# Cross attention and a routed feed-forward block: the attention loop's order of scores, maxima and projections

## The reference

```python
x = x + xattn(layernorm(x), ctx, ctx, mask, w_q, w_k, w_v, w_o)
x = x + ffn(layernorm(x), ...)          # causal attention, router, 2 of 8 experts

def xattn(q, k, v, mask, w_q, w_k, w_v, w_o):
    query, key_, value = (split_heads(t @ w.T) for t, w in ((q, w_q), (k, w_k), (v, w_v)))
    query, key_ = _rope(query), _rope(key_)
    scores = einsum('bhqd,bhkd->bhqk', query, key_) / sqrt(DK)
    scores = where(mask[:, None, None, :] == 0, -10000.0, scores)
    x = einsum('bhqk,bhkd->bhqd', softmax(scores), value)
    return merge_heads(x) @ w_o.T
```

## Time and profile before

| what | value |
| --- | --- |
| median of 3 runs | 823.15 us (822.39 to 824.36) |
| span of the profiled execution, first to last instruction | 808.3 us |
| around the span, against that median | 14.9 us |
| mean granted TensorE clock over the span | 0.940 |
| TensorE busy, of the span | 706.0 us, 87% |
| VectorE busy | 557.3 us, 69% |
| ScalarE busy | 485.6 us, 60% |
| GpSimd busy | 355.8 us, 44% |
| first score of g0 | 86.6 us from the span's start |
| start of the last score of g127 | 522.8 us |
| granted clock 0.5 inside the loop | 90.5 to 107.6, 216.8 to 220.2 and 411.3 to 418.2 us |

### The profile page before, as it was taken

How to read it: one execution, slowest core, us unless ns; L and a number is a source line. 1 busy time by engine, 2 the same in 40 slices (tenths; PEclk the granted TensorE clock), 3 DMA queues, 4 the chain that set the end, 5 groups by cost and what they waited for, 6 DMA issues and landing times. The chain is left out here.

```text
span 808.3 us, 13262 instructions
## 1 busy us (share of the span) xinstructions
PE 706.0 (87%) x4318; PEld 425.8 (53%) x4318; DVE 557.3 (69%) x924; ACT 485.6 (60%) x940; POOL 355.8 (44%) x262
## 2 busy tenths in 40 slices
PE   3246899999899999899999899888978889999996
PEld 2242434443344443435334333276767778999986
DVE  5949777778777778778878884248996515555553
ACT  2010556777576778567766678856655136676673
POOL 4964605358006277005749991000035723544444
PEclk9775689999999999999989999999998799999999
DMA  9676264868655666114777872039925646633321
GB/s 258 213 224 165 84 240 124 229 155 271 206 158 173 176 187 239 58 45 119 224 260 262 276 273 79 1 93 358 344 53 135 256 108 141 120 35 40 33 32 20
DMA packets 59718, 130.71 MB, mean 162 GB/s; under 512 B 8869, under 2 KB 26309, under 8 KB 58197
## 3 DMA queue, kind: packets, MB, share of 16 engines
q1 hardware_dynamic: 33364, 72.86, 27.6%
q0 software_dynamic: 16848, 35.95, 17.6%
q10 hardware_dynamic: 9440, 21.06, 9.0%
HBM read 80.80 MB, written 69.39 MB: 186 GB/s over the span
## 5 line engine op out<-in xcount | busy, mean ns | idle before, releaser
L757 DVE TENSOR_REDUCE mx<-wide 128x2 f32<-128x1024 f32 x256 | 305.6, 1223 | 89.0 <-PE wide L928 88.4
L616 ACT ACTIVATE probs<-narrow 128x512 f32<-128x512 f32 x488 | 267.3, 601 | 94.4 <-PE narrow L966 92.6
L966 PE MATMUL narrow<-qst,kst 51*128 51x512 f32 x488 | 182.9, 464 | 4.2 <-ACT probs L616 3.5
L928 PE MATMUL wide<-kst,qst 49*128 49x512 f32 x512 | 159.7, 476 | 21.4 <-DVE mx L757 9.4
L966 PEld LDWEIGHTS narrow<-qst,kst 51*128 51x128 f32 x488 | 78.9, 190 | 147.3 <-ACT probs L616 94.7
L981 PE MATMUL values<-probs,vaug 128*17 128x512 f32 x1024 | 139.2, 616 | 1.4 <-ACT probs L616 0.8
L1735 POOL DMA_INDIRECT out<-res,token x39 | 61.2, 1569 | 91.7 <-DMA out<-res,token 60.2
L928 PEld LDWEIGHTS wide<-kst,qst 49*128 49x128 f32 x512 | 68.6, 198 | 43.7 <-DVE mx L757 28.0
L462 POOL TENSOR_TENSOR turn_b<-turn_a,tab 128x1024 f32<-128x1024 f32 x10 | 24.2, 2420 | 115.3 <-ACT turn_a L610 114.8
L1267 POOL DMA_DIRECT2D out<-xt x4 | 5.5, 1376 | 108.1 <-DVE xt L1462 108.1
L1760 ACT ACTIVATE h_hi<-narrow 128x512 fp32r<-128x512 f32 x39 | 23.3, 598 | 42.2 <-PE narrow L1840 42.2
(11 more groups left out here) (281 smaller groups left out, 1310.4 us busy)
## 6 DMA issues: line engine op xcount, KB each, us to landing
list_rows<-in_w ACTq DMA_DIRECT2D x56, 342.0 KB, 5.5
kst<-k_pieces SPq DMA_DIRECT2D x14, 784.0 KB
k_pieces<-turn_a SPq DMA_DIRECT2D x16, 512.0 KB, 5.2
w_hi<-w_hi SPq DMA_DIRECT2D x16, 512.0 KB, 11.0
w_lo<-w_lo SPq DMA_DIRECT2D x16, 512.0 KB, 11.8
turn_a<-in_w POOLq DMA_DIRECT2D x11, 512.0 KB, 5.7
w_hi<-turn_b POOLq DMA_DIRECT2D x11, 512.0 KB, 3.0
w_lo<-turn_a POOLq DMA_DIRECT2D x11, 512.0 KB, 4.6
```

The source lines that it names most:

```text
L616: nc.scalar.activation(probs[:, n % NP, :], score_bank(n), ACT.Exp, scale=DK ** -0.5).then_inc(exp_done, 1)
L757: last = nc.vector.tensor_reduce(mx[quad % 2][:, qt, :, hp, kh], slot[:, :, :], axis=AX.X, op=ALU.max)
L928: last = nc.tensor.matmul(slot[:, i, :], qst[u % 3][r:r + R_MAX, h, P * qt:P * qt + P], kst[u % 3][r:r + R_MAX, h, 512 * kh:512 * kh + 512 ...
L966: nc.tensor.matmul(score_bank(n), kst[u % 3][r:r + R_ALL, h, P * kt:P * kt + P], qst[u % 3][r:r + R_ALL, h, :], start=True, stop=True).the ...
```

## The change

The order inside a group becomes s0, maximum, s1, weigh of g-1, s2, maximum, s3, then all other jobs; every group up to g116 has two maxima (g0 three, g117 none), and the last maxima of a quad end 3 groups before it for all quads. The estimated costs and `place` are gone. q, k, v and oP inside the loop come in halves of 256 columns, one to a group. xn, and the pieces of the turned attention, get buffers of their own (`xn`, `aT_hi`, `aT_lo`); the mask's two small tiles move into `attn` to make room. The unused `begin` and `finish` are taken out. In SP's queue the store of the turned queries goes ahead of the second max rows, and the loads of queries and keys ahead of the third.

```diff
-def lead(quad):
-    return 3 + 0.25 * max(quad - 5, 0)
-GROUP_COST = 2.3
-JOB_COST = {"q": 1.4, "k": 1.4, "v": 1.4, "oP": 1.4, "xT": 1.0, "oT": 1.0, "out": 0.5}
 AHEAD = 4
+LEAD = 3
...
-    for t in range(1, B):
-        g = 32 * (t - 1)
-        timed += [(g + 5.8, ("xn", t)), (g + 7, ("xT", t)), (g + 8.5, ("q", t, 0)), (g + 10, ("q", t, 1)), (g + 10, ("rope", t, 2))]
-        timed += [(g + x, ("v", t, n // 2, n % 2)) for n, x in enumerate((11.5, 13.5, 15, 16.5))]
-    for t in range(2, B):
-        g = 32 * (t - 2)
-        timed += [(g + 14.5, ("c", t, 0)), (g + 17.5, ("c", t, 1))]
-        timed += [(g + x, ("k", t, n // 2, n % 2)) for n, x in enumerate((18.5, 21, 23.5, 26))] + [(g + 21, ("rope", t, 0)), (g + 26, ("rope", t, 1))]
+    for b in range(B):
+        g, t = 32 * b, b + 1
+        if t < B:
+            timed += [(g, ("xn", t)), (g + 0.5, ("xT", t))]
+            timed += [(g + x, ("q", t, n // 2, n % 2)) for n, x in enumerate((3, 4, 6, 7))] + [(g + 7.5, ("rope", t, 2))]
+            timed += [(g + 13.2 + n, ("v", t, n // 4, n // 2 % 2, n % 2)) for n in range(8)]
+        if t + 1 < B:
+            timed += [(g + 16.5, ("c", t + 1, 0)), (g + 20.5, ("c", t + 1, 1))]
+            timed += [(g + 21.2 + n, ("k", t + 1, n // 4, n // 2 % 2, n % 2)) for n in range(8)] + [(g + 24.5, ("rope", t + 1, 0)), (g + 28.5, ("rope", t + 1, 1))]
+        if b > 0:
+            timed += [(g + 2.2, ("oT", b - 1))] + [(g + x, ("oP", b - 1, n // 2, n % 2)) for n, x in enumerate((8, 10, 11, 12))]
...
-    for b in range(B - 1):
-        g = 32 * b + 32
-        timed += [(g + 2.2, ("oT", b)), (g + 3.5, ("oP", b, 0)), (g + 5.5, ("oP", b, 1))]
...
-        first, last = when(max(8 * (quad - 1) - lead(quad - 1), 0)), when(8 * quad - lead(quad))
+        first, last = max(8 * (quad - 1) - LEAD, 0), 8 * quad - LEAD
...
-        timed += [(place(first + (last - first) * n / (len(todo) - 1)), j) for n, j in enumerate(todo[:-1])] + [(place(last) + 0.6, todo[-1])]
+        timed += [(first + (last - first) * n / (len(todo) - 2), j) for n, j in enumerate(todo[:-2])] + [(last - 0.01, todo[-2]), (last + 0.1, todo[-1])]
...
+        steps = [("score", 4 * g)] + [("job", j) for j in tops[:1]] + [("score", 4 * g + 1)] + [("weigh", g - 1)] * (g > 0)
+        steps += [("score", 4 * g + 2)] + [("job", j) for j in tops[1:2]] + [("score", 4 * g + 3)]
+        return steps + [("job", j) for j in tops[2:] + rest]
...
-    attn = sb("attn", [P, QT, D])
-    xn = attn
-    aT_hi, aT_lo = xT_hi, xT_lo
+    attn, xn = sb("attn", [P, QT, D]), sb("xn", [P, QT, D])
+    aT_hi = sb("aT_hi", [P, KC, SQ], F32R)
+    aT_lo = sb("aT_lo", [P, KC, SQ], F32R)
+    mask_i, mask_s = attn[0:B * KT, 0, 0:P].bitcast(I32), attn[0:B * KT, 1, 0:P]
...
             if t < B:
                 load_keys(2 * t)
+                store_turned(t, 2)
             load_max_rows(4 * b + 2)
             if t < B:
-                store_turned(t, 2)
+                load_queries(2 * t)
             if t + 1 < B:
                 load_context(t + 1, 1)
             if t < B:
-                load_queries(2 * t)
-            load_max_rows(4 * b + 3)
-            if t < B:
                 load_queries(2 * t + 1)
                 load_keys(2 * t + 1)
+            load_max_rows(4 * b + 3)
...
+                cols = columns(j[3:])
+                return product(slot[:, cols], weight("q", slice(P * j[2], P * j[2] + P)), transposed("xT", cols))
```

More of the change, by code:

```diff
@@ L33, with final @@
 HALF = 64
-def lead(quad):
-    return 3 + 0.25 * max(quad - 5, 0)
-GROUP_COST = 2.3
-JOB_COST = {"q": 1.4, "k": 1.4, "v": 1.4, "oP": 1.4, "xT": 1.0, "oT": 1.0, "out": 0.5}
 AHEAD = 4
+LEAD = 3
+def final(order, *begin):
+    return next(j for j in reversed(order) if j[:len(begin)] == begin)
 def attention_order():
@@ L67, in attention_order @@
     for quad in range(QUADS - 1):
-        timed.append((8 * quad + 9.3, ("out", quad)))
+        timed.append((8 * quad + 9.1, ("out", quad)))
     timed += [(GROUPS - 12.8, ("oT0", B - 1)), (GROUPS - 9.5, ("oP0", B - 1))]
-    for b in range(B - 1):
-        g = 32 * b + 32
-        timed += [(g + 2.2, ("oT", b)), (g + 3.5, ("oP", b, 0)), (g + 5.5, ("oP", b, 1))]
-    lengths = [GROUP_COST + sum(JOB_COST.get(j[0], 0) for t, j in timed if int(t) == g) for g in range(GROUPS)]
-    begins = [sum(lengths[:g]) for g in range(GROUPS + 1)]
@@ L108, in attention_order @@
     after += [("root0", 0), ("again0", 0), ("root0", 1), ("rates0", 0)]
-    order = before + [j for now in steps for what, j in now if what in ("job", "finish")] + after
+    order = before + [j for now in steps for what, j in now if what == "job"] + after
     index = {j: n for n, j in enumerate(order)}
@@ L112, in attention_order @@
     for b in range(1, B):
-        assert index[("xT", b)] < index[("out", 4 * (b - 1))]
-        assert b < 2 or index[("oT", b - 2)] < index[("xn", b)] and index[("oP", b - 2, 1)] < index[("xT", b)]
-        assert index[("q", b, 1)] < index.get(("oT", b - 1), len(order))
-        assert all(index[("v", b - 1, g, 1)] < index[("c", b, g)] for g in range(2))
+        assert index[("xT", b - 1)] < index[("xn", b)] and index[final(order, "q", b - 1)] < index[("xT", b)]
+        assert all(index[final(order, "v", b - 1, g)] < index[("c", b, g)] for g in range(2))
+        assert b < 2 or index[final(order, "oP", b - 2)] < index.get(("oT", b - 1), index.get(("oT0", b - 1)))
     return order, index, before, steps, after
@@ L230, in cross_attention @@
     for now in group_steps:
-        ring += [("score", j) if what == "score" else j for what, j in now if what == "score" or what in ("begin", "job") and in_ring(j)]
+        ring += [("score", j) if what == "score" else j for what, j in now if what == "score" or what == "job" and in_ring(j)]
     ring_no = {j: n for n, j in enumerate(ring)}
@@ L602, in job @@
                     act.wait_ge(pv_done, 32 * (b - 1))
[L603 to L604 removed]
+                kts = range(4 * g + 2 * n, 4 * g + 2 * n + 2)[slice(j[4], j[4] + 1) if j[4:] else slice(0, 2)]
+                dst, src = vaug[b % 2][:, kts.start:kts.stop, :, 0:DK], slot[:, columns(j[4:])].rearrange("p (k h d) -> p k h d", k=len(kts), h=H)
             else:
@@ L647, in _ @@
                     exponential_of_pair(g)
-                elif what in ("job", "finish"):
+                elif what == "job":
                     job(j)
@@ L821, in _, with product @@
         pe.wait_ge(ident_in, 16)
-        def product(out, left, right, part=None):
+        def product(out, left, right):
             passes = [(a, c, k) for a, c in ((0, 0), (0, 1), (1, 0)) for k in range(KC)]
             for n, (a, c, k) in enumerate(passes):
-                if part is None or n // KC in part:
-                    last = nc.tensor.matmul(out, left(a, k), right(c, k), start=n == 0, stop=n == len(passes) - 1)
+                last = nc.tensor.matmul(out, left(a, k), right(c, k), start=n == 0, stop=n == len(passes) - 1)
             return last
```

117 lines of the change are left out of this document (43 added, 74 removed).

## The result

The changed kernel is slower: 835.62 us median of 4 runs (830.53 to 838.24) against 822.77 (821.71 to 824.36), a ratio of 1.0169 with a 95% interval of 1.0129 to 1.0208. The forecast was 818.3, its range ended at 832.

The account below looks back on a forecast made before the run. Plain groups were taken as bound by a ring of weigh, scores and exponentials between TensorE and ScalarE, projection groups by TensorE. The parts summed to -4.8 us on the 823.15 us median, giving 818.3, range 804 to 832.

Parts of the forecast that it names:

- Part 4: xn and xT one behind the other at three places: two groups take 9.6 us instead of 5.3, in all +4.4.
- Part 8: Max rows queued behind stores of turned keys: late by 2.5 us at g32 and 1.2 at g64, +2.7.
- Part 9: TensorE's clock in the loop: three short low spells at xT, +1.5 us, between 0 and +13.6.
- what would show it: Signs to check in the new trace; a low clock in over 25 us of the loop would disprove the clock term.
- Rival (c): TensorE's stands of 2.5 us at xT bring low-clock spells of 17 us: 830.4 us, chance 0.12.
- Part 1: New order in a group: plain groups 2.65 instead of 2.59 us, +7.0; a slot saved at low clock, -1.7.
- Part 2: q, k, v projections in halves: 52 times 0.57 us instead of 26 times 1.32, -4.7; such a group takes 3.22.
- Part 3: Output's projection at batch ends: transposes 1.75 us, four quarters 1.05 each; three times -2.05, so -6.1.
- Part 5: Groups with out: 14 cost 15.5 us before; after, nine alone cost 1.05 each, five with a half 0.65: -2.8.
- Part 7: The loop's tail: last maxima come two groups later, so two more groups aren't paired, +0.9 us.
- Part 6: Maxima spread evenly over groups: less TensorE waiting for reductions, -6.0 us, between 0 and 12 taken back.
- 14.9 us around the span: Difference between before's 823.15 us median and its 808.3 us profiled span, taken as lying around the span and staying.

Follow-up runs that it names:

- xn_rows: Changed kernel with xn moved to where GpSimd is idle and each fourth quad's max row put ahead of the query and key loads: 804.90 us, 0.9811 of before.
- no_cast: xn_rows with the 16 small casts of the negated maxima computed as a second reduction: 802.43 us, 0.9739 of before.
- rows_first: Changed kernel with each batch's fourth-quad max row put back ahead of the loads of queries and keys: 826.37 us, 1.0068 of before.
- old_weave: xn_rows with each group's steps in the order of the kernel before: 843.97 us, 1.0260 of before.
- before_again: The kernel before, unedited, run again for a second profile: 820.25 us, ratio 1.0017 to before.
- xn_two_ahead: xn_rows with xn of batches 2 and 3 two groups ahead of their transposes, inside GpSimd's rotations again: 812.82 us, 1.0039 of before.

## Why the prediction was wrong

By its own parts:

- **Part 4, xn and xT, failed, and decided the sign.** The step was "the four normalisations take 1.37", a duration from a place where GpSimd was idle, carried to a place where it isn't. The two groups were to take 9.6 us; they took 17.5, 14.1 and 16.4, 19.2 us more in all three places together, part of it at the lower clock. Without the stand (xn_rows) they take 8.3, 7.6 and 8.0. The Trainium skill ("SBUF — State Buffer", Who interferes with whom) has the rule that would have told it: VectorE and GpSimd share one pair of SBUF ports as an exclusive lock for a whole instruction, and on VectorE's side copies, casts and tensor_scalar between SBUF tiles can take it, as does anything with two SBUF inputs against a GpSimd instruction that reads, while tensor_reduce never does. The traces agree in all four. Beside GpSimd tensor_scalar took up to 2.50 us instead of 0.40, the cast up to 2.14 instead of 0.18, the subtraction of two SBUF tiles up to 1.88 in no_cast instead of 0.18, and the reductions 0.19 and 1.21 to 1.23, as they do alone. Rows of the kernel before, the cast at 1.78 above, would have told it too.
- **Part 8, late rows, was mis-sized and in the wrong place.** I put 2.5 us at g32 and 1.2 at g64, for stores of turned keys; from these terms, less the 0.64 of before, the term is 3.1 and not the 2.7 written. The wait at g32 was 1.2 and there was none at g64. All such waits are 8.2 us: 5.9 of it at g24 (3.4), g56 (1.1) and g88 (1.4), the fourth quads of their batches, whose rows I had moved behind the loads without a price, and 1.2 at g104, whose cause is open. With the clock behind them, rows_first gets about 8 us back. I had said that the wait of the earlier trace rows speaks against completion out of order. A rule that allows it doesn't promise it: at g24 a row of 8 KB landed 9.9 us after its issue, behind 2.3 MB of loads. The same section of the Trainium skill ("DMA: Bandwidth & Descriptors", Queues, rings and completion order) says that each DMA engine takes its descriptors in the ring's order. The trace agrees: the row's packets move at 178.8 to 180.4, when the loads' end at 179.5. I had weighed one half of it.
- **Part 9, the clock, was mis-sized.** I allowed 1.5 us for three short spells; the low clock held in 44.4 us of the loop. It started from 17.0 us, the longest of the three spells of before, which are 27.4 together; so the limit of 25 in the "what would show it" list was passed by the kernel before itself and is no test. Rival (c) had the sign and a time of 830.4, but by stands of 2.5 us; the stands were of 5.6 to 8.2, and the cause is VectorE's.
- **Part 1, the interleave, was right for plain groups** (2.65 after, 2.59 in old_weave) and blind to what the order is worth beside other jobs: with the halves, the old order costs 38 us in the loop. Of these, 15.1 are shown to come from the transposes between the first two scores, which hold up all scores when their input is late; the other 22.7 aren't taken apart. The -1.7 at the low clock isn't seen by itself; the one plain group that stands almost wholly at that clock, 96 in xn_rows, took 3.76, where before took 4.04 and the forecast was 3.61.
- **Part 2, halves**: 3.20 to 3.23, forecast 3.22. But the gain doesn't come from halving: whole pieces in the new order cost the same to 0.4 us. The term has about its size, and names the wrong edit as its cause; that the forecast per group came out is no proof of the reason given.
- **Part 3**: the attention's transposes cost 3.87 - 2.65 = 1.2 (1.75 forecast), the four quarters 4.0 (4.2). **Part 5**: out costs 1.15 alone with its neighbour (1.05) and 0.5 with a half (0.65). **Part 7** is 2.0 where I had 0.9: the two more unpaired groups, 116 and 117, took 3.0 and 3.4, not 2.65.
- **Part 6** isn't seen by itself. But parts 1, 2, 3, 5, 6 and 7 sum to -13.4, and xn_rows, where the two stalls are away but xT's own cost stays, is at -12.5 against before_again and -19.5 against the earlier trace rows.
- The **"14.9 us around the span"** were no such thing: 1.9 is around it, and the profile of before was quicker than its runs. Adding the 14.9 did no harm to the forecast, since it cancels out to 823.15 - 4.8, but it hid that the profile and the runs were of different executions.

So 835.6 is 818.3 with about 19 us more for part 4 and 4.9 more for part 8 (8.2, less the 0.64 of before, for 2.7), the clock partly in both. That is 7 us too much. Against the loop of before_again (430.7) the sum fits better: -4.8 + 19.2 + 4.9 = 19.3, measured 19.9. But that is in part luck, since the profiled execution of the changed kernel lies 2.6 us above its median and that of before_again 1.8 below its own; no step of mine holds the rest, and the loop of one and the same kernel varies by as much. What is sure is the sign: take the two stalls away and the same change is 1.9% faster than before (1.4 to 2.4%).

## What to carry to other kernels

A duration read from a trace holds only beside the same neighbours: before an instruction of VectorE between SBUF tiles is moved, look at what GpSimd does at the new place, and count up to a whole GpSimd instruction for each of them. In these traces only reductions, and operations with an operand in PSUM, took the same time beside GpSimd as alone. Distance to the reader doesn't help, since what waits is the queue behind (xn_two_ahead). A small DMA that something waits for goes ahead of the big ones that are ready earlier, even if it isn't ready when they are: in this kernel SyncE had ten idle microseconds to wait in.

## What the runs showed of the hardware that I had not expected

- VectorE's four subtractions in a row get in only once between two GpSimd instructions: with GpSimd's queue full, one VectorE instruction of 0.40 us passes per GpSimd instruction of 2.34, and xn takes 6.83 to 7.91 us instead of 1.37. Where fewer or shorter GpSimd instructions stand beside it, it takes 4.3 and 5.2. GpSimd's own long instructions keep their 2.34 to 2.41 (2.35 to 2.43 in the loop of before); the whole price is VectorE's. The busy time in the profile counts the wait as work, which is how 18 us of "busy" VectorE came without instructions.
- A cast of 16 columns can take 2.14 us. It is the smallest instruction on the path and cost more than the reduction of 1024 columns.
- The operations on PSUM beside it weren't touched: the reductions of 128x1024 took 1.21 to 1.23 us throughout, and so did the subtraction for xT's low piece, which reads one tile of PSUM and one of SBUF, 1.22 to 1.23.
- The part behind the loop, which no run changes, takes 286 and 287 us in the two profiles of one chip and 296 to 297 in those of the two others. That the loop is alike on them is inferred: before as a whole is 11 to 14 us quicker on that chip, and this part is about 10 of it.
